# A new order for the steps of a recurrent layer's token mixer: one full step re-ordered on four engines, and a first step whose mixes wait for less

## What is computed

```python
dx = x_last - x;  xm = x + dx * x_miu
mix = tanh(xm @ x_A)                      # six groups of 32
r_in, w_in, k_in, v_in, a_in, g_in = x + dx * (lambdas + mix @ x_B)
v = v_in @ vW.T;  r = r_in @ rW.T;  g = tanh(g_in @ g_A) @ g_B
w = -softplus(-(w_miu + tanh(w_in @ w_A) @ w_B)) - 0.5
k = normalize(k_in @ kW.T + tanh(k_in @ k_A) @ k_B)
a_gate = sigmoid(a_time + a_in @ a_A @ a_B) * 2
# per token and head, state S is 64 x 64:
S = S * exp(w) + (S @ -k) b^T + v kk^T ;  y = S @ r
out = (groupnorm(y) * gamma + beta + bonus) * g @ oW.T
# experts: each token's two best of 8 share wi and wo, and differ in a rank-16 addition to wi
```

## Time and profile before

| | |
|---|---|
| runs | 992.45, 993.99, 994.77 us; median 993.99 |
| profiled execution | 991.9 us, span 989.7 us |
| busy in the span | PE 975.6 (99%), DVE 835.0 (84%), ACT 635.2 (64%), POOL 442.0 (45%) |
| step 1 | 0 to 34.91 us |
| step 2 | 34.91 to 95.21 us |
| steps 3 to 16 | 95.21 to 938.70 us, about 60.1 us each |
| step 17 | 938.70 to 989.7 us |

### The profile page before, as it was taken

One profiled execution on the slowest core, in us unless ns is written; L12 is line 12 of the kernel. 1 busy time (PEld: TensorE's weight loads), 2 busy tenths in 40 slices (PEclk: granted clock), 3 DMA queues, 4 the chain that ended last, 5 costly groups with the idle time before them and its releaser, 6 DMA issues.

```text
span 989.7 us, 46754 instructions
## 1 busy us (share of the span) xinstructions
PE 975.6 (99%) x20570; PEld 769.4 (78%) x20570; DVE 835.0 (84%) x1684; ACT 635.2 (64%) x1481; POOL 442.0 (45%) x537
## 2 busy tenths in 40 slices
PE   8999999999999999999999999999999999999997
PEld 5777778787787877778877787877878777787775
DVE  5887979889798897979979798797988979789776
ACT  3665666656657566675666666566575665756655
POOL 3461734537244371634617345272442715436150
PEclk9999999999999999999999999999999999999999
DMA  7000000000000000000000000000000000000000
GB/s 261 13 3 3 3 4 23 4 24 4 4 24 4 23 5 23 3 4 23 4 24 4 3 25 3 23 4 3 24 4 24 3 25 3 3 24 4 13 4 23
DMA packets 9416, 17.28 MB, mean 17 GB/s; under 512 B 1920, under 2 KB 4224, under 8 KB 8960
## 3 DMA queue, kind: packets, MB, share of 16 engines
q1 hardware_dynamic: 9216, 14.30, 4.4%
HBM read 10.10 MB, written 4.19 MB: 14 GB/s over the span
## 4 chain that ended last, share of the span: by engine, by line
PE 96%; ACT 2%; DVE 1%; issue 1%; ACTq 0%; DVEq 0%
PE bank L255 34%; PE bank L254 20%; PE grams L470 10%; PE bank L348 5%; PE bank L485 3%; PE bank L496 3%; PE grams L539 2%; PE grams L444 2%; PE grams L594 2%; PE grams L559 2%; PE bank L570 2%; PE bank L363 2%; PE bank L529 2%; PE bank L379 2%; PE bank L580 1%; PE bank L303 1%
## 5 line engine op out<-in xcount | busy, mean ns | idle before, releaser
L1265 POOL TENSOR_TENSOR bk<-bk,tot 128x256 f32<-128x256 f32 x192 | 155.1, 815 | 137.1 <-PE grams L470 137.1
L1583 DVE COPY_PREDICATED gm<-c_mask_g,grams 128x1024 f32<-128x1024 int32 x96 | 161.4, 1681 | 6.1 <-PE grams L470 4.3
L1021 ACT ACTIVATE gl<-gm 32x128 f32<-32x128 f32 x320 | 99.1, 310 | 79.1 <-DVE gm L1583 72.9
L1246 POOL TENSOR_TENSOR xd<-mtmp,xnc 128x512 f32<-128x512 f32 x96 | 122.3, 1275 | 14.4 <-DVE mtmp L1449 12.6
L914 ACT ACTIVATE relu<-bank,prm 128x256 f32<-128x256 f32 x256 | 105.6, 471 | 36.1 <-PE bank L255 33.6
L470 PEld LDWEIGHTS grams<-ar,bk 64*64 64x64 f32 x6144 | 102.0, 134 | 19.8 <-issue 14.8
L255 PE MATMUL bank<-w_wo,hid 128*128 128x256 f32 x488 | 116.1, 386 | 0.0
L470 PE MATMUL grams<-ar,bk 64*64 64x64 f32 x6144 | 110.2, 220 | 0.0
L1593 DVE TENSOR_TENSOR ar<-ar,tot 128x512 f32<-128x512 f32 x96 | 92.3, 962 | 13.2 <-PE grams L470 13.2
L255 PEld LDWEIGHTS bank<-w_wo,hid 128*128 128x128 f32 x488 | 90.2, 190 | 13.1
L255 PE MATMUL bank<-xnc,w_wi 128*128 128x256 f32 x392 | 94.4, 384 | 0.9 <-ACT relu L914 0.9
(11 more groups left out here) (241 smaller groups left out, 2149.0 us busy)
## 6 DMA issues: line engine op xcount, KB each, us to landing
x_in<-x SPq DMA_DIRECT2D x16, 256.0 KB, 2.8
out<-out_t SPq DMA_DIRECT2D x15, 256.0 KB, 2.0
w_wi<-w_wi_dram SPq DMA_DIRECT2D x1, 1024.0 KB, 6.8
w_wo<-w_wo_dram SPq DMA_DIRECT2D x1, 1024.0 KB, 8.8
w_lora_B<-w_lora_B_dram SPq DMA_DIRECT2D x1, 512.0 KB, 7.6
w_x_B<-w_x_B_dram SPq DMA_DIRECT2D x1, 384.0 KB, 3.2
w_kW<-w_kW_dram SPq DMA_DIRECT2D x1, 256.0 KB, 3.8
w_rW<-w_rW_dram SPq DMA_DIRECT2D x1, 256.0 KB, 4.3
```

The lines of the kernel that those rows point to most:

```text
L1021: A(gl[l % 2][o:o + 32, :, :, :].rearrange("p q g (c n m) -> p (q g c) n m", c=2, m=m), right(gm[o:o + 32, :, :, :, b, 0, 32 * k:32 * k + ...
L1246: tt(xd[:, q, :, :], mtmp[:, k % 2, :, :], xnc[steps["front"] % 2][:, :, :], ALU.add).then_inc(S(f"xd_{k}_done"), 1)
L1265: tt(v, v, d, ALU.mult).then_inc(S(f"bk{k}_scaled"), 1)
L1583: run(v.copy_predicated(dst, msk.to_broadcast([128, 32, HALF // m, m]), src), "g_stored")
```

## The change

```diff
-        mtmp = sb("mtmp", [128, 2, 2, G * L])
+        mtmp = sb("mtmp", [128, 4, 2, G * L])
...
+        def mixes_in(pair):
+
+            return (bank[0], bank[2]) if steps["front"] == 0 and pair == 1 else MIU
...
             def miu(pair):
-                pe.wait_ge(*till("mixt_done", 5))
+                pe.wait_ge(*till("mixt_done", 5 if pair == 1 else 1))
...
                         route()
+                        warm(2)
+                        mix()
                         warm(1)
-                        mix()
-                        warm(2)
                         if step == 1:
                             wait_loaded(pe, 1)
                         miu(0)
-                        warm(3)
+                        pe.wait_ge(*till("xnc_done", 1))
+                        pe.wait_ge(*till("route_read", 1))
+                        miu(1)
+                        warm(2)
                         pe.wait_ge(*till("mx_0_done", 2))
                         pe.wait_ge(*till("mx_1_done", 2))
-                        miu(1)
+                        miu(2)
+                        wk_A()
                         kW(half=True)
-                        wk_A()
+                        pe.wait_ge(*till("mx_2_done", 2))
+                        wk_B()
...
+                        g_B(half=True)
+                        warm(1)
                         pe.wait_ge(*till("hg_done", 1))
+                        a_B(half=True)
+                        pe.wait_ge(*till("r_done", 1))
+                        xmt_()
+                        pe.wait_ge(*till("ha_done", 1))
                         v_()
...
-                    pe.wait_ge(*till("xmt_done", 0))
+                    pe.wait_ge(*till("v_done", 0))
...
                         rt_e()
+                        mixt_e()
+                        mixt_f()
                         exps()
-                        mixt_e()
                         hwk()
+                        sig_()
+                        kraw_()
                         hg()
-                        kraw_()
+                        nrm_()
                         ha()
-                        sig_()
+                        gate_(step)
+                        r_e()
                         agate_()
-                        nrm_()
-                        r_e()
-                        gate_(step)
+                        xmt_e()
                         ar0(rec)
-                        xmt_e()
                         v_e(rec)
...
-                if k >= 2:
-                    dve.wait_ge(*till(f"xd_{k - 2}_done", 1))
+                if k >= 4:
+                    dve.wait_ge(*till(f"xd_{k - 4}_done", 1))
...
+            def mixed_sum(k):
+                q = MIX_ORDER[k]
+                dve.wait_ge(*till(f"mx_{k}_done", 2))
+                run(v.tensor_tensor(xd[:, q, :, :], mtmp[:, k % 4, :, :], xnc[steps["front"] % 2][:, :, :], ALU.add), f"xd_{k}_done")
```

More of the change, by code:

```diff
@@ L654, in tile @@
-                        pe.wait_ge(*till("mx_3_done", 2))
-                        miu(2)
                         pe.wait_ge(*till("kraw_done", 1))
                         pe.wait_ge(*till("ksq_done", 1))
[L658 to L661, removed]
+                        norm(half=True)
+                        pe.wait_ge(*till("sig_done", 2))
+                        g_B(half=True)
@@ L753, in tile @@
                             pe.wait_ge(*till("xmt_done", 0))
-                        route(half=True)
+                        route()
+                    if rec:
+                        gram(1)
+                        diff(1, half=True)
+                    if front:
                         pe.wait_ge(*till("xnc_done", 1))
@@ L757, in tile @@
                     if rec:
-                        diff(0, half=True)
-                        base(3, half=True)
+                        base(2, half=True)
+                        gram(2)
                     if front:
@@ L766, in tile @@
                     if rec:
-                        gram(2)
                         inv_x(1)
-                        base(2)
+                        base(3)
+                        lora(2)
                         lora(3)
-                        inv_off(1)
                     if front:
@@ L777, in tile @@
                         gram(3)
-                        inv_x(2)
+                        inv_off(1)
                     if front:
@@ L782, in tile @@
                     if rec:
-                        lora(2, half=True)
-                        inv_off(2)
+                        diff(3, half=True)
+                        inv_x(2)
                     if front:
@@ L789, in tile @@
                     if rec:
+                        inv_off(2)
+                        down(1, first=True)
                         gram(4)
-                        diff(3)
+                        inv_x(3)
                     if front:
@@ L795, in tile @@
                     if rec:
-                        inv_x(3)
+                        inv_off(3)
                     if front:
@@ L806, in tile @@
                         pe.wait_ge(*till("ksq_done", 1))
-                        g_A()
+                        norm(half=True)
+                        pe.wait_ge(*till("sig_done", 2))
+                        a_A()
+                    if rec:
+                        inv_off(4)
+                        diff(2)
+                        if front:
+                            pe.wait_ge(*till("nrm_done", 1))
+                        elif full:
+                            pe.wait_ge(*till("gate_done", 0))
+                        keys_to_tokens(0)
+                        top_x()
+                        rec_p(0)
+                        top_off()
                     if post:
                         if front:
-                            pe.wait_ge(*till("sig_done", 2))
+                            pe.wait_ge(*till("ha_done", 1))
                         elif full:
@@ L1802, in tile @@
                     if rec:
-                        hidden(1)
+                        store(2)
+                        hidden(0)
                     if front:
@@ L1807, in tile @@
                     if rec:
+                        scale_ar(2)
                         keep_x(1)
-                        scale_ar(2)
-                        store(2)
-                        add_off(1)
+                        hidden(1)
                     if front:
```

252 lines of the change are left out of this document (106 added, 146 removed).

## The result

The changed kernel takes **995.26 us** (994.74 to 998.08, 20 runs) where the kernel before, run beside it, takes 993.27 us (991.82 to 996.07, 20 runs): a ratio of 1.0018 with a 95% interval of 1.0012 to 1.0025. It is slower, as forecast, but by 2.0 us and not by 6.4 (1000.4 less 993.99, the median of three runs that the forecast started from), and it sits at the bound of 0.2% rather than clearly beyond it. The profiled execution took 995.24 us with a span of 993.3 us, 3.6 us more than the span before.

The account below looks back on a forecast made before the run. TensorE's stream of products was taken to bound the full steps: 2.8 + 5.0 + 6.3 - 1.9 - 1.2 - 3.6 = +7.4 on 991.9 gives 999.3, with half the offset 1000.4 us; own range 997 to 1003, with rivals 990 to 1006.

Parts of the forecast that it names:

- Term 1: TensorE, full steps: 37 changes of array tile instead of 36, +0.20 us per step, 14 times, +2.8 us.
- Term 2: TensorE, full steps: rec_inc(1) waits for Scalar's copy sa_out(1), +0.36 us per step, 14 times, +5.0 us.
- Term 3: TensorE, full steps: wk_A waits for Vector's third mix, delayed by GpSimd's sums; +0.45 us per step, +6.3 us.
- Term 4: Instruction-supply stops in inv_x(4) go, as dense products now separate the small-tile blocks: -1.9 us, bounds 0 to -4.
- step 2: Loses an instruction gap and rec_inc(1)'s wait for the copied keys: -1.2 us, bounds -2.2 to 0.
- step 1: Earlier miu(0), wk_A and diag despite one more table load; step 2 starts at 31.3 instead of 34.91: -3.6 us.
- last step: Keeps its order, left unchanged by the prediction.
- carried offset: Median of runs before is 2.1 us above their profiled execution; half carried, taking 999.3 to 1000.4 us.
- GpSimd does not hold Vector at hidden(1): Rival, 22 in 100: GpSimd's sum of mix 0 begins after hidden(1), so term 3 is gone: 993.6 us.
- Neither wait comes: Rival, 13 in 100: rec_inc(1) also finds its input, for instance because Scalar's copy starts earlier: 988.2 us.
- More waits: Rival, 18 in 100: norm late by 0.3 us and g_B by 0.1, 15 times, +6: 1006.4 us.

Follow-up runs that it names:

- g_A_between: The kernel before with dense product g_A moved between gram(5) and inv_x(4) in steps 2 to 16: 993.40 us, ratio 0.9999 to the kernel before.
- both_ahead: hidden_ahead plus down(3) moved ahead of rec_inc(1) in the full steps alone: 987.37 us, ratio 0.9938 to the kernel before.
- inc_behind_down: The changed kernel with down(3) in halves moved ahead of rec_inc(1), behind bonus: 991.87 us, ratio 0.9984 to the kernel before.
- hidden_ahead: The changed kernel with Vector's hidden(1) right behind hidden(0), ahead of the first two mixes, in steps 2 to 16: 991.85 us, 0.9982 to the kernel before.
- mix0_one: The changed kernel with GpSimd's sum for mix 0 cut to one column in steps 2 to 16: 991.92 us, ratio 0.9981 to the kernel before.
- before_again: The kernel before, unchanged, profiled a second time: 992.98 us, span 990.8 us.
- first_only: The kernel before with only the first step changed, with its banks and the four temporaries: 990.59 us, ratio 0.9971 to the kernel before.
- hidden_first: The changed kernel with Vector's hidden(1) swapped ahead of keep_x(1) in steps 2 to 16: 998.49 us, ratio 1.0046 to the kernel before.

## Why the prediction was right and wrong

The direction, the mechanisms and the places were right; the size was not: the forecast time is 5.1 us too high (1000.4 against 995.3; the range of 990 to 1006, wide because of its rivals, holds it, the forecast's own of 997 to 1003 does not), and the loss was forecast three times as large as it is (6.4 against 2.0 us). The terms, predicted against the profiled execution and measured between the two spans:

| term | predicted | measured | from |
|---|---|---|---|
| 1 change of tile | +2.8 (0.20) | +2.2 (0.16) | g_A_between, both_ahead |
| 2 rec_inc(1) | +5.0 (0.36) | +5.0 (0.36) | rows of after, inc_behind_down |
| 3 wk_A | +6.3 (0.45) | +3.4 (0.24) | rows of after, hidden_ahead |
| 4 instruction gaps | -1.9 | -2.5 in the first trace (-4.1 and -4.5 in two others) | step lengths |
| step 2 | -1.2 | -1.35 | windows |
| step 1 | -3.6 | -3.2 | windows |
| last step | 0 | +0.1 | windows |
| sum | +7.4 | +3.6 | |

Of the 5.1 us, 3.8 are in this sum, 1.05 in the carried offset (below), and 0.3 lie outside the spans (2.2 us before, 1.9 after). The 6.4 us of slowdown are too much by 4.4, and not by 5.1, because the three runs of before that the forecast started from had a median 0.7 above that of the 20.

**Term 3 is the step that failed in size: 2.9 of the 3.8 us by which the sum was too high.** "That ends at +22.7, and wk_A starts 0.45 late" adds the chain of Vector up from rounded pieces: first mix +17.0, second sum over at +21.2, 0.6, 0.85. Measured: +17.2, +21.1, then 0.5 to the next start and 0.86, which is +22.45. The block positions on TensorE's side were exact to a tenth (gram(1) +8.8, gram(2) +13.95, miu(0) +14.9, miu(1) +19.9, wk_A unhindered +22.27). The wait is the small difference of two large positions, so an error of 0.2 us in one of them halves it. The hold itself was right; mix0_one and hidden_ahead show it by taking it away from both sides.

**Term 2** was exact, since it rests on one rigid chain of three rows, not on a sum over 22 us. **Term 1** was 0.04 a step too high. The rows gave 0.10 for entering the full array and 0.10 for leaving it; the sum left out that one direct change between two small tiles goes at the same time, so the 0.16 is a difference, and no run shows which of its parts is smaller than taken.

**Term 4 and the carried offset are the second failure, 0.6 and 1.05 us.** The main place and the cause stood up: with a dense product between the small blocks the stops in inv_x(4) are gone (after, g_A_between). Its size did not. The sum took the three stops that show as "issue" in inv_x(4) for all of them, but steps are also lengthened at wk_A, at diff(3) and at gram(5), by 0.05 to 0.7 us a time. "This is the only place where one packet's worth runs in under 2 us" is so by start times (1.9 us), but stops also came where one runs in 2.5 us, around wk_A. "The median of the runs before is 2.1 above their profiled execution. Part of that may be instruction gaps, which go; I carry half": nothing should have been carried. In after, without the gaps, the profiled execution (995.24) and the median (995.26) agree; in the nine kernels without the stops in inv_x(4) the median lies from 0.5 us below to 0.6 above the profiled execution, while before's lies 1.4 above (993.27 against 991.9). The profiled execution of before had drawn little of them: 2.5 us in its full steps against 4.1 and 4.5 in two other traces of that order, where the median is only 0.9 and 0.2 above. That the whole offset is gaps is the likely reading, and was not shown execution by execution. The offset is also why the medians differ by 2.0 us and the two spans by 3.6, but for the 0.3 outside the spans.

**Step 1** went as worked out: miu(0) at 12.21 (forecast 12.2), miu(1) at 13.24 (13.3), wk_A at 16.35 (16.4), one table load more and hidden in part; diag came at 30.52 (29.9) since bonus waited for dg2 until 29.85, and base(1) at 31.67 (31.3). **Step 2** was right. The change is said to let miu(0) and miu(2) wait for the first tanh only; in the full steps a wait for all five stands ahead of miu(0) in both kernels, so there this edit frees nothing, and its gain is in step 1 alone.

**The rivals.** "GpSimd does not hold Vector at hidden(1)" (993.6) did not come, though the total lies nearer to it than to the forecast: the full step is 60.83 us, above the 60.6 that I had named as its mark, and the hold is in the rows. "Neither wait comes" fell by the same rows. "More waits" fell too: no third wait in after, and none in both_ahead behind the two. What would have shown the forecast wrong has not appeared; 61.1 us for the full step was 0.25 too much (0.21 of the wait, 0.04 of the tile).

By the page's rule on instruction fetch that the prediction weighed (the Trainium skill, Runtime: NRT & Kernel Launch, "Instruction fetch mechanics": the next block is fetched while the current one runs, mostly hidden), term 4 is nothing. The traces of before, before_again and first_only show otherwise for this kernel, with 2.5 to 4.5 us in 14 steps.

## What to carry to other kernels

A wait that is the difference of two long chains should be given a range as wide as the error of either chain, and a likeliest value in the middle of it; one that rests on a short rigid chain can be given to the hundredth. When a profile shows stops that belong to no engine, take the profile as one draw: here the main places recurred in a second execution and the sizes did not, and the distance from the profiled execution to the median is likely to be theirs. Where one engine's instruction holds another's, as GpSimd's sums held Vector here, an earlier start within the hold gained nothing (hidden_first), and a place ahead of what feeds the other engine gained the whole wait (hidden_ahead): move it there. And look whether a block moved in all steps was filling a wait in one of them: down(3) was, in step 2.

## What the hardware showed that was not expected

- A Vector addition with both inputs in SBUF, started 0.2 us earlier into GpSimd's sums, ended no earlier: 1.56 us became 1.75, and both ended 0.55 us behind the second sum. Of two sums in a row GpSimd let one such instruction through in between (scale_ar(2), 1.19) and lost about 0.4 us by it (2.95 for two, where one takes 1.27).
- The largest stops in supply recur in the same steps from one execution to the next (step 15: 0.77 and 1.03 us idle) with other sizes, and end 1.2 to 1.5 us after a packet of the instruction queue. One dense product of about 1 us between the small blocks ended those in inv_x(4) and left 0.8 us of 2.5 to 4.5 (g_A_between); in after the full steps have none.
- One more way into the full array and out of it, in place of a direct change between small tiles, costs 0.16 us, to the hundredth the same in two different orders (60.23 us in g_A_between and in both_ahead).
